# Attention's turned weights: one copy of eight heads against two copies of four, each with its own bank and signal

## What is computed

```python
x = _layernorm(x + _L0_attn_ref(x, ...))        # four Mamba blocks
x = _layernorm(x + _L0_xattn_ref(ctx, ctx, x, mask, ...))   # cross attention, 16 heads of 8
x = _layernorm(x + _L0_ffn_ref(x, ...))         # product-key experts
x = _layernorm(x + _L1_attn_ref(x, ...))        # trajectories
x = _layernorm(x + _L1_xattn_ref(x, ctx, ...))  # self attention over top-k scores, cross attention, FFN
x = _layernorm(x + _L1_ffn_ref(x, ...))         # gated layer with quantised weights
```

```python
scores = jnp.einsum('bhqd,bhkd->bhqk', q, k) * scale
attn = jax.nn.softmax(scores, axis=-1)      # self attention: only the 5 largest scores of a row
out = jnp.einsum('bhqk,bhkd->bhqd', attn, v)
out @ wo.T + bo
```

## Time and profile before

| what | value |
|---|---|
| median of 3 runs | 8483.58 us (8464.3 to 8492.16) |
| the profiled execution's own time | 8499.55 us |
| its span, first to last instruction | 8497.5 us |
| mean granted clock of TensorE | 0.843 of full speed |
| busy: PE, DVE, ACT, POOL | 76%, 79%, 52%, 57% of the span |
| cross attention of layer 0 | from about 4220 to 4940 us |
| decoder stage | from about 6370 to 8115 us |

### The profile page before, as it was taken

One profiled execution on the slowest core, in us unless ns is written; L12 is line 12 of the kernel. 1 busy time (PEld: TensorE's weight loads), 2 busy tenths in 40 slices (PEclk: granted clock), 3 DMA queues, 4 the chain that ended last, 5 costly groups with the idle time before them and its releaser, 6 DMA issues. The chain is left out here.

```text
span 8497.5 us, 93901 instructions
## 1 busy us (share of the span) xinstructions
PE 6487.2 (76%) x25844; PEld 3454.5 (41%) x25859; DVE 6694.5 (79%) x15635; ACT 4390.8 (52%) x8810; POOL 4876.1 (57%) x2829
## 2 busy tenths in 40 slices
PE   5888888888888888888788867777556777777745
PEld 2333333333333333333355545555434545555532
DVE  5999999999999999999755558888667666666657
ACT  3555555555555555555455523333226666666633
POOL 4888878888888878888644434444222333333310
PEclk8898889899898899898898978888658988888855
DMA  5333333334333333333300046767310000000011
GB/s 184 133 148 155 137 149 155 132 148 160 133 148 155 132 153 151 137 148 155 112 25 22 20 132 204 208 201 206 92 47 7 10 9 9 9 9 9 6 31 36
DMA packets 373728, 896.56 MB, mean 106 GB/s; under 512 B 28031, under 2 KB 270076, under 8 KB 306972
## 3 DMA queue, kind: packets, MB, share of 16 engines
q1 hardware_dynamic: 332508, 692.64, 21.7%
q0 software_dynamic: 40960, 201.36, 8.3%
HBM read 850.58 MB, written 56.77 MB: 107 GB/s over the span
## 5 line engine op out<-in xcount | busy, mean ns | idle before, releaser
L380 POOL TENSOR_TENSOR mb_dBu<-mb_dtu,mb_rows_b 128x1024 f32<-128x1024 f32 x1027 | 2405.7, 2359 | 363.3 <-DVE mb_bank L394 186.6
L394 DVE TENSOR_TENSOR_SCAN mb_bank<-mb_bank,mb_dBu 128x1024 f32<-128x1024 f32 x704 | 1612.8, 2291 | 72.0 <-PEq L63 50.9
L434 PE MATMUL mb_bank<-mb_hcd,ident 128*128 128x512 f32 x2560 | 1271.6, 624 | 78.9 <-DVE mb_hcd L408 78.8
L365 ACT ACTIVATE mb_bank<-mb_dt,mb_a_neg 128x508 f32<-128x508 f32 x2050 | 1315.1, 673 | 0.8
L434 PE MATMUL mb_bank<-mb_hcp,ident 128*128 128x512 f32 x1280 | 796.7, 755 | 355.0 <-POOL mb_hcp L417 355.0
L417 POOL TENSOR_TENSOR mb_hcp<-mb_hs,mb_rows_c 128x1024 f32<-128x1024 f32 x320 | 752.8, 2352 | 360.0 <-DVE mb_hs L394 359.7
L408 DVE TENSOR_TENSOR mb_hcd<-mb_bank,mb_rows_c 128x1024 f32<-128x1024 f32 x704 | 862.1, 1225 | 31.3
L434 PEld LDWEIGHTS mb_bank<-mb_hcd,ident 128*128 128x128 f32 x2560 | 502.1, 203 | 798.3 <-issue 591.3
L1537 POOL DMA_INDIRECT ex_rows<-in_ex_table,ex_idx x512 | 490.3, 958 | 561.3 <-DVE ex_idx L1533 331.9
L394 DVE TENSOR_TENSOR_SCAN mb_hs<-mb_bank,mb_dBu 128x1024 f32<-128x1024 f32 x320 | 730.9, 2284 | 42.2 <-ACT mb_bank L365 42.2
L434 PEld LDWEIGHTS mb_bank<-mb_hcp,ident 128*128 128x128 f32 x1280 | 284.8, 236 | 806.1 <-POOL mb_hcp L417 480.1
(11 more groups left out here) (369 smaller groups left out, 13327.9 us busy)
## 6 DMA issues: line engine op xcount, KB each, us to landing
mb_rows_b<-bc_rows SPq DMA_DIRECT2D x259, 1024.0 KB, 7.6
mb_rows_c<-bc_rows SPq DMA_DIRECT2D x258, 1024.0 KB, 6.8
stream<-mb_r_post SPq DMA_DIRECT2D x69, 256.0 KB, 2.4
mb_r_tok<-stream SPq DMA_DIRECT2D x67, 256.0 KB, 2.8
mb_r_post<-stream SPq DMA_DIRECT2D x65, 256.0 KB, 2.9
ex_rows<-in_ex_table,ex_idx POOLq DMA_INDIRECT x512
tj_x_tok<-stream SPq DMA_DIRECT2D x17, 256.0 KB, 3.0
bc_rows<-mb_xp SPq DMA_DIRECT2D x65, 64.0 KB, 1.6
```

What stands on the lines that cost most here:

```text
L365: e = nc.scalar.activation(da_of(n)[:, c * GB:(c + 1) * GB, 1:], dt[q][:, c].rearrange("p (b t) -> p b t", b=GB)[:, :, 1:], ACT.Exp, scale ...
L380: nc.gpsimd.tensor_tensor(by_c(dBu[m % RING][:]), by_c(chains(dtu[q][:])), over_c(rows_b[:, n]), ALU.mult).then_inc(s["mb_dbu"], 1)
L394: nc.vector.tensor_tensor_scan(flat(to), flat(da_of(n)), flat(dBu[n % RING][:]), 0.0, ALU.mult, ALU.add).then_inc(s["mb_scan"], 1)
L434: m = nc.tensor.matmul(bank[:, B_Y + c], ident[:], part[:, c * GB:(c + 1) * GB], start=False, stop=False)
```

## The change

`act_turned` makes two instructions of 512 elements a partition out of one of 1024: the first copies bank 4, the second bank 5. Each waits for its own count of "tr" and counts up "pt". `pe_turn` counts up "tr" after each four heads, and its second four wait for the second count of "pt" of the unit before. `pe_values` waits for the first "pt" ahead of head 0 and for the second ahead of head 4. `upto` counts "tr" and "pt" twice for each unit.

```diff
+HALVES = ("shift", "tr", "pt")
...
-                total += 2 if name == "shift" else 1
+                total += 2 if name in HALVES else 1
...
     def pe_turn(self, pe, t):
         nk = self.unit(t).nk
         self.wait(pe, "pick" if self.topk(t) else "exp", t)
-        self.wait(pe, "pt", t - 1)
-        for h in range(HH):
-            m = self.nc.tensor.transpose(self.bank[0:nk, 4 + h // 4, (h % 4) * P:(h % 4 + 1) * P], self.e_of(t, nk)[:, h], self.ident[:])
-        m.then_inc(self.sem("tr"), 1)
+        for j in range(2):
+            self.wait(pe, "pt", t - 1, less=1 - j)
+            for h in range(4):
+                m = self.nc.tensor.transpose(self.bank[0:nk, 4 + j, h * P:(h + 1) * P], self.e_of(t, nk)[:, 4 * j + h], self.ident[:])
+            m.then_inc(self.sem("tr"), 1)
...
-        self.wait(pe, "pt", t)
         if half == 0:
             self.wait(pe, "ot", n - 1)
         for h in range(HH):
+            if h % 4 == 0:
+                self.wait(pe, "pt", t, less=1 - h // 4)
...
     def act_turned(self, act, t):
         nk = self.unit(t).nk
-        self.wait(act, "tr", t)
         self.wait(act, "pv", t - 2)
-        self.nc.scalar.activation(self.pt[t % 2][0:nk].rearrange("p (j h) q -> p j (h q)", j=2), self.bank[0:nk, 4:6],
-                                  ACT.Copy).then_inc(self.sem("pt"), 1)
+        for j in range(2):
+            self.wait(act, "tr", t, less=1 - j)
+            self.nc.scalar.activation(self.pt[t % 2][0:nk, 4 * j:4 * j + 4].rearrange("p h q -> p (h q)"), self.bank[0:nk, 4 + j],
+                                      ACT.Copy).then_inc(self.sem("pt"), 1)
```

## The result

| | before | after |
|---|---|---|
| median of 6 runs each | 8482.36 us (8464.3 to 8494.33) | 8398.27 us (8381.88 to 8414.59) |
| ratio, 95% interval | | 0.9907 (0.9894 to 0.9921) |
| span of the profiled execution | 8497.5 us | 8406.3 us |
| mean granted clock of TensorE | 0.843 | 0.856 |

What follows compares the result with a forecast made beforehand. The prediction took a ring of TensorE, `ots`, weight copy and values to bound the cross attentions. Its terms, 9.5 + 15.1 + 2 - 1 = 25.6 us, were cut to 23, giving 8460 us, range 8430 to 8494.

Steps and rivals of the forecast that it cites:

- What bounds the kernel: Both attention stages: TensorE's stream nearly fills layer 0's cross attention, 622 of 720 us; late weight copies cost it waits.
- The ring: Cross attentions: time runs from TensorE through `ots`, weight copy and values back to TensorE; time cut out there is gained.
- (1) The copy: ScalarE's copy of turned weights: two halves cost 0.06 us more a unit, bounds nothing to 0.19 us.
- (2) The values: TensorE's value steps with late copy: net saving 0.13 us each at full clock, 0.25 us at half clock.
- (3): TensorE's turn: its second four heads wait for the second copy of the unit before; cost nothing.
- (4): "tr" after four heads: ScalarE may start about 0.5 us earlier, 63 times; counted as nothing, at most 25 us.
- The sum: Both attention stages: 9.5 + 15.1 + 2 - 1 = 25.6 us saved, cut to 23 us; 39 of 206 waits at half clock.
- Larger gain: Rival, 36 to 65 us: each wait gives up to 0.32 us, or the earlier "tr" counts; chance 0.16.
- The clock: Rival in self attention: longer idle before the pick brings more half clock, 39 us slower, 8523 us; chance 0.11.
- No gain: Rival, -12 to +12 us: halves start about 0.60 us apart without overlap, or the ring doesn't end rounds; chance 0.19.
- What would show it: Profile after: halves 0.48 us apart, values in two lots, `ot` wait 0.13 shorter, `pt` wait some 25 us less, busy time unchanged.

Runs made afterwards that it cites:

- e1: Changed kernel with the two half copies, but "tr" counted once and the values waiting for both halves ahead of head 0: 8448.99 us, ratio 1.0004.
- e6: Kernel before plus twelve unread transposes on TensorE at the start of each round of layer 0's cross attention: 8412.68 us, ratio 0.9943.
- e7: Changed kernel plus twelve unread transposes on TensorE at the start of each round of layer 0's cross attention: 8360.37 us, ratio 0.9878.
- e3: Kernel before plus eight unread transposes on TensorE ahead of each turn's wait for the pick in self attention: 8425.99 us, ratio 0.9973.
- e4: Changed kernel plus eight unread transposes on TensorE ahead of each turn's wait for the pick in self attention: 8389.06 us, ratio 0.9926.
- e2: Changed kernel with "tr" counted once for each unit and both half copies waiting for the whole turn: 8385.94 us, ratio 0.9927.
- e5: Changed kernel measured again as it is, on another chip: 8396.21 us, ratio 0.9924.
- e9: Kernel before plus an unread ScalarE copy of 512 elements at the start of each round of layer 0's cross attention: 8479.28 us, ratio 1.0010.
- e8: Changed kernel with the first values of each round in layer 0 waiting for both halves: 8392.03 us, ratio 0.9921.
- e10: Changed kernel plus an unread ScalarE copy of 896 elements at the start of each round of layer 0's cross attention: 8409.83 us, ratio 0.9927.
- e13: Changed kernel with the first four value steps of each round of layer 0's cross attention waiting for both halves: 8400.98 us, ratio 0.9911.
- e14: Changed kernel with the last four value steps of each round of layer 0's cross attention waiting for both halves: 8415.33 us, ratio 0.9934.

## Why the prediction was wrong in its size

Step by step, as the prediction numbers them.

- **What bounds the kernel.** The ring was right, and so was that TensorE's stream is nearly all of layer 0. What it drew from this, that time cut out of the ring is gained, held. That the length of TensorE's stream also depends on how much of it runs at half clock was left aside here.
- **(1) The copy.** Right. Price 0.06 us: 1.07 for the pair against 1.01, 0.07 a wait in e1. The Trainium skill's budget (ScalarE: Activation LUTs, Rules for kernel authors) of about 0.3 us for each ACTIVATE is stated for a bias given as a pointer operand, which these copies do not have; as the price of one more copy behind another the trace decides against it.
- **(2) The values.** Right, slightly low: 0.16 us from rows against 0.13. By the full-clock rounds of e6 and e7 layer 0 gains some 11 us, not 9.5; e3 and e4 give 11 us in the decoder stage where 16 were forecast, and in the cross attention of 14 rounds the kernels with the overlap stand 9 to 13 us under the line of those without it. Together some 22 us for the forecast's 23. The saving of a late copy at half clock, 0.25 in the forecast, was not measured by itself.
- **(3) and (4), the turn and "tr".** Right: no cost appears, and e2 gives back nothing.
- **The sum.** Here it failed: it has no term for the half-clock time of the rest of TensorE's stream. It took 39 of the 206 waits to be at half clock and priced them, as if the other products would run at the clock that they had, and so put the change of that time at nothing without a reason. In layer 0 half-clock time fell from 163 us to 118 and, in e5, 96. At the 0.46 us that e6 gained for each microsecond, 45 to 67 fewer make 21 to 31 us, and the stage gained 25 to 33 us over the ring's 11. In the decoder stage it is the cross attention that gained. There the profiles with the old copy and the old order have 143, 99 and 82 us at half clock (before, e9, e6), the changed kernel's 48, 48 and 55 (after, e5, e7). At 0.37 us each that is 35 us between before and after, and 21 us between the means, 108 and 50. The whole stage is at 1801 to 1826 us in the former and at 1770 to 1780 in seven profiles with the overlap, the old order and no filler there (after, e5, e7, e8, e10, e13, e14). The missing term is so 21 to 33 us in layer 0 and 21 to 35 in the decoder stage; with the 22 us of the ring that makes 64 to 90 us, where 67 and 84 were measured.
- **The rivals.** "Larger gain" had the sign and not the cause: it came by neither 0.32 us for each wait nor the earlier "tr". The clock was a rival only as a loss, and only in self attention, where it counts for little: those stretches are as long with 157 us at half clock (e7) as with 123 (after), 641 and 642 us. That it falls after idle still agrees with the rows, but here the change of timing took half-clock time away, and the prediction gave that side no chance. "No gain" did not arise: the second half starts 0.48 us behind the first by the pair's 1.07.
- **What would show it.** The halves, the two lots, the shorter wait of `ot` and the load after it all came as described. Two lines did not. TensorE's wait for `pt` fell by 26 + 59 = 85 us and not by 25: a value step starts some 0.4 us sooner and then stands still inside, so this list counts more than the ring gains. And "busy time stays" did not hold, which gives the error away: busy PE fell by 12 and 23 us with not an instruction removed, though the values themselves grew.

Shown is that half clock cost some 50 us in layer 0 (e6, an edit that only adds products nobody reads), that without the overlap nothing is gained as a whole (e1), that in the decoder stage the gain lies in the cross attention, and that in layer 0 the later steps of a round matter (e14) and the early ones don't (e8, e13). That half-clock time is lower with the change is seen in each of its profiles without filler, in layer 0 (96 to 118 us against 147 to 163) and in the decoder's cross attention. Why it is stays open: no run shows what in those later steps decides whether the clock falls, and no single step was undone in the decoder stage. Nor is half clock there set by the code alone, since the same cross attention has 143, 99 and 82 us of it in three profiles. The stage lengths are of one profile each, on chips whose other stages differ by up to some 40 us in sum, and two profiles of the changed kernel differ by 8 us in layer 0, so terms below that are not told apart.

## What to carry to other kernels

Where TensorE sets the pace and its granted clock is below 1, a sum over waits is incomplete: give the clock a term of its own, with both signs, and size it by the half-clock time that may come or go, here at 0.37 to 0.46 us for each microsecond. The list of waits alone misleads when a split moves part of a wait inside a group. To judge a small overlap, first hold the clock with products that nobody reads, before and after, and compare rounds at clock 1.00. And ahead of splitting a copy that comes late, look at what it stands behind on its engine: moving it ahead of a copy that was still waiting was worth more (0.9882) than the split (0.9907 and 0.9924), part of both by way of the clock, and the two together still more (0.9845).

## What the runs showed of the hardware

Rounds of one program settle into patterns of clock and length that repeat. In the decoder stage of before, nine rounds in a row take 109.2 us. Windows of TensorE show an earlier round of 104 us and one of the nine:

```profile
6764.30:6868.30 104.00, 75.98 (x574) 0.91 0.03 9
...
7087.60:7196.80 109.20, 81.14 (x575) 0.84 0.03 9
```

The same work takes 5.2 us longer and TensorE is busy 5.2 us more, at clock 0.84 instead of 0.91. In layer 0 the pattern was 39.2, 43.0, 41.1, 44.1 in one profile of the changed kernel and 38.8 and 43.1 in turn in the other (e5), with 44.3 to 44.6 from the sixth round on in e1 and e9. Adding 12 transposes to a round of some 44 us made it up to 5 us shorter.
